# Keys of the later batches formed by channel instead of by transposing normalised tokens

## The reference

```python
k  = layernorm(x)                      # over channels; keys
# for each batch and channel, over the tokens t in order:
y  = (A*p + E*v) / (A*q + E)           # WKV recurrence with decay w and bonus u
x2 = x + tanh(g_xattn) * y
z  = layernorm(x2).astype(f16)
d  = gelu(z @ W0.T + bias0).astype(f16)   # 1024 -> 4096
e  = (d @ W1.T + bias1).astype(f16)       # 4096 -> 1024
out = x2 + tanh(g_ffn) * e
```

## Time and profile before

| | us |
|---|---|
| median of 3 runs | 1995.39 (1993.98 to 1995.86) |
| the profiled execution | 1994.41 |
| its span | 1992.6 |
| PE busy | 1856.8 (93%) |
| DVE busy | 847.7 (43%) |
| ACT busy | 549.8 (28%) |
| POOL busy | 261.9 (13%) |

### The profile page before, as it was taken

The page is one execution under the profiler, slowest core; times in us unless marked ns, Lnnn a source line. Parts: engine busy times, 40 slices in busy tenths (PEclk is TensorE's granted clock), DMA queues, the critical chain, the costliest instruction groups (busy, mean ns, idle before and its releaser), DMA issues.

```text
span 1992.6 us, 20961 instructions
## 1 busy us (share of the span) xinstructions
PE 1856.8 (93%) x8960; PEld 878.9 (44%) x8960; DVE 847.7 (43%) x998; ACT 549.8 (28%) x647; POOL 261.9 (13%) x202
## 2 busy tenths in 40 slices
PE   0069998899999999999999999999999999999999
PEld 0034444344544444444444444444444444444444
DVE  6978779686433666631223776642111000000000
ACT  3139744434422433410001443420100221210000
POOL 2335411334330011000000101000000000000000
PEclk9989999999999999999999999999999999999999
DMA  5727837578353442442233334323322222123330
GB/s 195 253 81 277 313 132 266 209 252 311 115 177 138 143 161 96 142 182 98 93 127 122 114 129 164 137 96 116 127 92 87 96 85 85 64 85 127 127 116 32
DMA packets 76748, 287.12 MB, mean 144 GB/s; under 512 B 7920, under 2 KB 7920, under 8 KB 69488
## 3 DMA queue, kind: packets, MB, share of 16 engines
q1 hardware_dynamic: 75648, 285.24, 40.5%
q10 hardware_dynamic: 1008, 0.55, 0.1%
HBM read 218.66 MB, written 67.11 MB: 143 GB/s over the span
## 4 chain that ended last, share of the span: by engine, by line
PE 81%; DVE 10%; issue 3%; DMA 3%; ACT 2%; POOL 1%; SPq 0%; ACTq 0%; DVEq 0%; POOLq 0%
PE acc L658 43%; PE acc L636 35%; DVE S L525 3%; PE front L608 1%; DVE stats L456 1%; DMA W<-parts_dram 1%; DVE S L511 1%; DVE S L514 1%; PE front L585 1%; PE back L617 1%; ACT L380 1%; POOL X L328 1%; DMA xin<-x_in 1%; DVE xin L472 1%; DMA b<-bias_in 1%
## 5 line engine op out<-in xcount | busy, mean ns | idle before, releaser
L636 PE MATMUL acc<-XT,W 128*128 128x512 f16 x4096 | 900.3, 381 | 17.5 <-DMA W<-parts_dram 12.0
L658 PE MATMUL acc<-DT,W 128*128 128x512 f16 x4096 | 892.5, 379 | 0.0
L636 PEld LDWEIGHTS acc<-XT,W 128*128 128x128 f16 x4096 | 401.6, 98 | 495.9 <-issue 13.6
L658 PEld LDWEIGHTS acc<-DT,W 128*128 128x128 f16 x4096 | 400.1, 98 | 471.6
L536 DVE SCALAR_TENSOR_TENSOR xo<-e,tg,xo 128x512 f32<-128x512 f16 x64 | 50.0, 783 | 654.3 <-ACT e L419 654.3
L411 ACT ACTIVATE DT<-acc,b 128x512 f16<-128x512 f32 x256 | 175.7, 687 | 546.1 <-PE acc L636 545.6
L419 ACT ACTIVATE e<-acc,b 128x512 f16<-128x512 f32 x64 | 43.9, 686 | 616.8 <-PE acc L658 616.8
L525 DVE RECIPROCAL S<-front 128x512 f32<-128x512 f32 x62 | 207.5, 3347 | 0.0
L328 POOL TENSOR_TENSOR X<-X,S 128x512 f32<-128x512 f32 x64 | 77.6, 1213 | 641.3 <-DVE S L528 641.3
L509 DVE TENSOR_TENSOR front<-front,V 128x512 f32<-128x512 f32 x62 | 43.2, 696 | 203.6 <-ACT front L380 203.6
L456 DVE BATCH_NORM_STATS2 stats<-front 128x6 f32<-128x512 f32 x64 | 41.4, 688 | 198.0 <-PE front L608 198.0
(11 more groups left out here) (50 smaller groups left out, 617.0 us busy)
## 6 DMA issues: line engine op xcount, KB each, us to landing
W<-parts_dram SPq DMA_DIRECT2D x56, 2048.0 KB, 8.5
parts_dram<-W SPq DMA_DIRECT2D x64, 512.0 KB, 6.1
stage<-w_in SPq DMA_DIRECT2D x52, 512.0 KB, 6.0
xin<-x_in SPq DMA_DIRECT2D x32, 512.0 KB, 6.1
V<-vT_in SPq DMA_DIRECT2D x64, 256.0 KB, 5.0
X<-xT_in SPq DMA_DIRECT2D x64, 256.0 KB, 3.0
x_dram<-X SPq DMA_DIRECT2D x32, 512.0 KB, 3.9
xo<-x_dram SPq DMA_DIRECT2D x32, 512.0 KB, 4.1
```

What stands on the lines that cost most here:

```text
L636: mm = nc.tensor.matmul(acc[m % BANKS][:, :], W[:, (nb // Q) % 2, part, nb % Q, P * c:P * (c + 1)], XT[:, c, HALF * half:HALF * (half + 1) ...
L658: mm = nc.tensor.matmul(acc[m % BANKS][:, :], W[:, s % 2, part, q, P * c:P * (c + 1)], DT[:, nb, HALF * half:HALF * (half + 1)], start=(nb ...
```

## The change

For batches 1 to 3 the key of a unit is formed from xT, which is loaded by channel anyway for the residual, and from a row that holds each token's mean and factor, the same for all partitions. The statistics are taken as before, tile by tile, but nothing is normalised by token: the pair (mean, factor) of 128 tokens is stored in a DRAM tensor, and after four tiles the row of 1024 numbers is loaded with a broadcast to all partitions, into `xin[2]` or `xin[3]`, which are free now. `keys(n)` on DVE subtracts, multiplies and adds the token-dependent term from a ramp; the different start of the second half goes into the exponential's shift. The transposes of units 16 to 63 are gone from PE. The first half's tiles of batch 1 move from slots 33 to 36 to slots 25 to 28 and the others are spread over every second slot; x is loaded two tiles ahead in two buffers; xT has eight landing semaphores instead of four. The first batch stays as it was.

```diff
     for i in range(HT):
         LN1_SLOT[HT + i] = 1 + i
-        LN1_SLOT[2 * HT + i] = 33 + i
-        LN1_SLOT[3 * HT + i] = 60 + i
+        LN1_SLOT[2 * HT + i] = 25 + i
+        LN1_SLOT[3 * HT + i] = 47 + 2 * i
...
-        LN1_SLOT[2 * TILES + i] = 107 + i
+        LN1_SLOT[2 * TILES + i] = 104 + 2 * i
...
-            LN1_SLOT[T + HT + i] = at + 33 + i
+            LN1_SLOT[T + HT + i] = at + 20 + 2 * i
             if b + 2 < B:
-                LN1_SLOT[T + TILES + i] = at + 119 + i
+                LN1_SLOT[T + TILES + i] = at + 112 + 2 * i
...
+    for n in range(UNITS, UNITS * B):
+        KEY_SLOT[n] = UNIT_SLOT[n] - 2 if n % UNITS == 0 else UNIT_SLOT[n - 1]
...
             def load_x(T):
-                half, slot = T // HT, T % HT
-                if half:
-                    sp.wait_ge(kt_done, CB * half)
+                half, slot = T // HT, T % HT if T < TILES else T % 2
+                if 0 < half < 4:
+                    sp.wait_ge(kt_done, CB * min(half, 2))
+                if T >= TILES + 2:
+                    sp.wait_ge(bn_done[0], 2 * (T - 1))
                 sp.dma_start(xin[:, slot, :], x[T]).then_inc(x_landed[slot], 16)
+
+            def store_norms(T):
+                sp.wait_ge(rstd_done[0], T + 1)
+                sp.dma_start(norms_dram[T // HT, T % HT], mv[:, 0, T % 2, :]).then_inc(norms_stored[T % 2], 16)
+
+            def load_norms(half):
+                for i in range(2):
+                    sp.wait_ge(norms_stored[i], 16 * (half - 1) * HT // 2)
+                if half >= 4:
+                    sp.wait_ge(k_ready, CB * (half - 3))
+                row = norms_dram[half:half + 1].rearrange("o a p k -> o (a p k)")
+                sp.dma_start(xin[:, 2 + half % 2, :], row.to_broadcast([P, 2 * HALF])).then_inc(norms_landed[half % 2], 16)
...
             def load_xT(n):
-                if n >= 4:
-                    sp.wait_ge(x2_done, n - 3)
+                if n >= 8:
+                    sp.wait_ge(x2_done, n - 7)
...
+                    if K - 1 in LN1_AT and LN1_AT[K - 1] >= TILES:
+                        T = LN1_AT[K - 1]
+                        store_norms(T)
+                        if T + 2 < TILES * B:
+                            load_x(T + 2)
+                        if T % HT == HT - 1:
+                            load_norms(T // HT)
...
+                    if K == LN1_SLOT[TILES]:
+                        pool.wait_ge(xn_ready, TILES)
+                        nc.gpsimd.iota(ramp, [[-1, HALF]], base=0, channel_multiplier=0, ...
...
             def exps(n):
-                act.wait_ge(kt_done, n + 1)
+                if n < UNITS:
+                    act.wait_ge(kt_done, n + 1)
+                else:
+                    act.wait_ge(k_ready, n - UNITS + 1)
...
             def stats_of(i, T, halves, free):
-                if T >= 2:
+                if i == 0 and T >= TILES + 2:
+                    dve.wait_ge(norms_stored[T % 2], 16 * ((T - TILES) // 2))
+                elif T >= 2:
                     dve.wait_ge(free, T - 1)
...
+            def keys(n):
+                b, i, c, half = n // UNITS, n % UNITS, n % CB, n // CB
+                E = unit_banks(n)[0]
+                m, r = norms[half % 2][:, :, 0], norms[half % 2][:, :, 1]
+                if i == 0:
+                    dve.wait_ge(xh_ready, TILES * b)
+                    dve.wait_ge(ramp_ready, 1)
+                else:
+                    dve.wait_ge(y_done, n - 1)
+                dve.wait_ge(xT_landed[n % 8], 16 * (n // 8 + 1))
+                dve.wait_ge(norms_landed[half % 2], 16 * (half // 2))
+                at = n - UNITS + 1
+                nc.vector.tensor_tensor(E, X2[:, i, :], m, ALU.subtract).then_inc(kc_done, 1)
+                dve.wait_ge(kc_done, at)
+                nc.vector.tensor_tensor(E, E, r, ALU.mult).then_inc(ks_done, 1)
+                dve.wait_ge(ks_done, at)
+                nc.vector.scalar_tensor_tensor(E, ramp, wp[:, c:c + 1], E, ALU.mult, ALU.add).then_inc(k_ready, 1)
...
                     if K + 1 in LN1_AT:
                         stats_x(LN1_AT[K + 1])
-                    if K in LN1_AT:
+                    if K in LN1_AT and LN1_AT[K] < TILES:
                         norm_x(LN1_AT[K])
+                    for n in KEYS_AT.get(K, ()):
+                        keys(n)
                     for n in UNITS_AT.get(K, ()):
                         unit(n)
...
             def tokens_x2(T):
-                pe.wait_ge(x2_done, UNITS * b + CB * (h + 1))
+                pe.wait_ge(x2_done, UNITS * b + (UNITS if b else CB * (h + 1)))
...
                     for n in UNITS_AT.get(K, ()):
-                        unit(n)
+                        if n < UNITS:
+                            unit(n)
```

More of the change, by code:

```diff
@@ L35 @@
 LN2_SLOT = {}
+KEY_SLOT = {}
 def place_front():
@@ L56, in place_front @@
         for i in range(HT):
-            LN1_SLOT[T + HT + i] = at + 33 + i
+            LN1_SLOT[T + HT + i] = at + 20 + 2 * i
             if b + 2 < B:
-                LN1_SLOT[T + TILES + i] = at + 119 + i
+                LN1_SLOT[T + TILES + i] = at + 112 + 2 * i
         for i in range(TILES):
             LN2_SLOT[T + i] = (at + 72 + 6 * i, at + 75 + 6 * i)
+    for n in range(UNITS, UNITS * B):
+        KEY_SLOT[n] = UNIT_SLOT[n] - 2 if n % UNITS == 0 else UNIT_SLOT[n - 1]
 place_front()
 UNITS_AT = {k: [n for n in UNIT_SLOT if UNIT_SLOT[n] == k] for k in set(UNIT_SLOT.values())}
+KEYS_AT = {k: [n for n in KEY_SLOT if KEY_SLOT[n] == k] for k in set(KEY_SLOT.values())}
 LN1_AT = {k: T for T, k in LN1_SLOT.items()}
@@ L88, in build @@
     x2_view = x2_dram.rearrange("b (h c) p u t -> b c u p h t", h=2)
+    norms_dram = nc.dram_tensor("norms_dram", (2 * B, HT, P, 2), F32).ap()
     parts_dram = nc.dram_tensor("parts_dram", (2 * STEPS, P, 2 * Q * 1024), F16).ap()
@@ L108, in build @@
         w_u, wn, decay = sb("w_u", [P, 2, CB]), sb("wn", [P, CB]), sb("decay", [P, CB])
-        wp, uu, bonus, shift = sb("wp", [P, CB]), sb("uu", [P, CB]), sb("bonus", [P, CB]), sb("shift", [P, CB])
+        wp, uu, bonus, shift = sb("wp", [P, CB]), sb("uu", [P, CB]), sb("bonus", [P, CB]), sb("shift", [P, 2, CB])
         grow = sb("grow", [P, H])
@@ L113, in build @@
         xin = sb("xin", [P, HT, H])
+        norms = [xin[:, 2 + i, :].rearrange("p (t k) -> p t k", k=2) for i in range(2)]
+        ramp = grow[:, 0:HALF]
         stats, mv, rstd = sb("stats", [P, 2, 2, 6]), sb("mv", [P, 2, 2, 2]), sb("rstd", [P, 2, 2, 2])
@@ L139, in build @@
         xn_done, xn_ready, xh_ready = sem("xn_done"), sem("xn_ready"), sem("xh_ready")
+        norms_stored, norms_landed, ramp_ready = sems("norms_stored"), sems("norms_landed"), sem("ramp_ready")
+        kc_done, ks_done, k_ready = sem("kc_done"), sem("ks_done"), sem("k_ready")
         kt_done, e_ready, y_done, x2_done = (sem(n) for n in ("kt_done", "e_ready", "y_done", "x2_done"))
@@ L180, in load_xT @@
                     sp.wait_ge(x2_stored[(b - 1) % 2], 16 * CB * ((b - 1) // 2 + 1))
-                sp.dma_start(X2[:, i, :], xT[b, i]).then_inc(xT_landed[n % 4], 16)
+                sp.dma_start(X2[:, i, :], xT[b, i]).then_inc(xT_landed[n % 8], 16)
             def store_x2(n):
@@ L282, in _ @@
                             store_x2(n - 1)
-                        if n % CB == CB - 1 and (n + 1) // CB < 2 * B:
-                            for T in range((n + 1) // CB * HT, ((n + 1) // CB + 1) * HT):
+                        if n == UNITS - 1:
+                            for T in range(TILES, TILES + 2):
                                 load_x(T)
@@ L319, in rstd_of @@
                 pool.wait_ge(ve_done[i], T + 1)
-                nc.gpsimd.tensor_tensor(rstd[:, i, T % 2, 1:2], rstd[:, i, T % 2, 0:1], power[:, :], ALU.pow)\
+                to = mv[:, 0, T % 2, 1:2] if i == 0 and T >= TILES else rstd[:, i, T % 2, 1:2]
+                nc.gpsimd.tensor_tensor(to, rstd[:, i, T % 2, 0:1], power[:, :], ALU.pow)\
                     .then_inc(rstd_done[i], 1)
@@ L325, in residual @@
                 pool.wait_ge(y_done, n + 1)
-                pool.wait_ge(xT_landed[n % 4], 16 * (n // 4 + 1))
+                pool.wait_ge(xT_landed[n % 8], 16 * (n // 8 + 1))
                 slot = X2[:, n % UNITS, :]
@@ L349, in _ @@
                         rstd_of(0, LN1_AT[K + 1])
+                    if K == LN1_SLOT[TILES]:
+                        pool.wait_ge(xn_ready, TILES)
+                        nc.gpsimd.iota(ramp, [[-1, HALF]], base=0, channel_multiplier=0,
+                                       allow_small_or_imprecise_dtypes=True).then_inc(ramp_ready, 1)
                     if K in X2T_AT:
@@ L374, in exps @@
             def exps(n):
-                act.wait_ge(kt_done, n + 1)
+                if n < UNITS:
+                    act.wait_ge(kt_done, n + 1)
+                else:
+                    act.wait_ge(k_ready, n - UNITS + 1)
                 if n == 0:
                     act.wait_ge(s_dve0, 6)
```

(13 more changed lines are left out.)

2 lines of the change are left out of this document (1 added, 1 removed).

## The result

The changed kernel takes 2004.59 us (median of 5 runs, 2004.06 to 2008.80) against 1995.39 (5 runs, 1992.79 to 1995.93): a ratio of 1.0055, 95% interval 1.0040 to 1.0069, so 0.55% slower. The profiled execution took 2006.68, its span is 2004.9.

A forecast was written before the change was run, and what follows sets the result against it. The prediction took TensorE as the bound (81% of the chain), with DVE holding it up in batch 0. Batch 0 17.7 us later less 16.7 saved gave +1.0, so 1996 us; range 1981 to 2013.

The forecast's parts named there:

- Batches 1 and 2: Later batches: removed transposes (14.1 us) and two waits for keys (2.6) save 16.7 us, 8.3 per batch; DVE's passes stay hidden.
- The port: SBUF port in each unit: DVE's first keys pass starts 0.04 us ahead of GpSimd's residual and wins, at no cost.
- the rival: GpSimd wins the port: first keys pass ends 1.08 us later, +14, about 2010; 25% together with slow passes.
- Slots 24 to 37: Batch 0: moved statistics and x loads make tile 4 5.3 us late, PE 8.7 late; slot 37 at 282.7.
- Slots 37 to 64: Batch 0: DVE without a gap, units 10.9 us apart; weights put slot 60 at 382.3, slot 64 at 398.6.
- Slots 64 to 88: From slot 64 of batch 0: DVE's gaps used up; tokens_x2(8) starts at 489.9, PE waits 8.4 us, clock costs 2.7.
- My fourth case: Something else is late too, a lo_piece before keys passes or the row of means: 2015 and above, 7%.
- The sum: Whole kernel: batch 0 17.7 us later, less 16.7 saved, is +1.0 us; forecast by the median 1996.
- the 498 named as the limit: Sign of being wrong: slot 88 comes by 480 or after 498 us.
- the stall of batch 0: Batch 0 up to slot 88: the change makes it 15.0 us later, before 2.7 more for the clock.
- the lost port: Case of GpSimd winning the port, or slow keys passes: about 2010 us, slower than before, 25%.
- a rival of 6 to 8 us: Smaller stall of batch 0: slot 60 and all behind it 6 to 8 us earlier, about 1987; 28%.

The follow-up runs named there:

- e2: The kernel before with eight landing semaphores for xT instead of four and nothing else: 1977.06 us against 1994.81, ratio 0.9912.
- e1: The changed kernel with keys by channel for batches 2 and 3 only, batch 1's by transposes at the old slots: 1963.77 us, ratio 0.9845.
- e6: The changed kernel with one more, unused DVE keys pass per unit in batches 2 and 3 only: 2004.58 us, ratio 1.0047.
- e8: The changed kernel with the wait for the unit before (`y_done`) named last instead of first in `keys`: 2011.06 us, ratio 1.0076.
- e11: The changed kernel with batch 1's keys formed in one pass, mean and factor left out, the wait for their row kept: 1995.83 us, ratio 1.0009.
- e3: The changed kernel with x of tiles 8 to 11 loaded at once into four buffers: 1998.43 us, ratio 1.0019.
- e4: The changed kernel with batch 0's weight loads issued ahead of the V loads in the SP queue: 1998.07 us, ratio 1.0021.
- e12: The changed kernel with the edits of e11, e3 and e4 together: 1984.43 us, ratio 0.9949.
- e5: The changed kernel with one more, unused DVE keys pass per unit in batch 1 only: 2014.54 us, ratio 1.0095.
- e7: The changed kernel with x of tiles 8 to 11 loaded at once and their statistics at slots 31 to 34: 2000.89 us, ratio 1.0028.

## Why the prediction was right or wrong

**Batches 1 and 2: right.** Predicted 16.7, less 2.7 for the clock behind slot 88, so 14.0 from `tokens_x2(8)` to the end; measured 15.15, and PE waits for nothing there. The two batches gained 9.0 and 8.0 (8.3 each was predicted), the clock behind slot 88 cost 1.8. The transposes are 7.0 of it in each batch (459.57 in e2, 452.59 in e1); the two waits are gone in e2 too, where the keys are as before, so the semaphores alone remove them. e6 shows that DVE's passes are hidden.

**The port: right.** DVE wins at a lead of 0.04 in the ordinary unit, and e8 shows the price if it does not: 6.5, about half of the 14 of the rival. The Trainium skill's rule (SBUF — State Buffer, "Who interferes with whom"), that whichever is issued first keeps the ports, agrees with 298.90 and 298.94 here, and with e8. It doesn't agree with e11, where the instruction that starts 0.04 earlier by the trace is the one held up; there the measurement decides. Of the two rows that the prediction held against the rule, the copy has only one SBUF input, so the part on two inputs says nothing of it.

**Slots 24 to 37: right in kind, short in size.** Tile 4 was to be 5.3 late; the rows of after run 1.4 earlier before this point (unit 15 ends at 229.87 against 231.24; in e2 tile 4 is 1.8 earlier, so the semaphores do that), and 236.52 - 232.74 + 1.4 is 5.2. Slot 29 was to be at 250.1 and came at 252.96: the loads of tiles 10 and 11 took 7.0 and 10.1 us, not 5.4. I had taken 5.4 from batch 1, where no weights are prepared; the chain of after shows the load (start us, us, what):

```profile
237.39 10.08 DMA xin<-x_in
```

Behind the 6 us wait the granted clock fell (0.52 from 253 to 257 us; it cost 1.9), which I had counted only at slots 60 and 88. Slot 37 came at about 287.4 instead of 282.7.

**Slots 37 to 64: right, with small terms too low.** Unit period 10.96 against 10.9. The waits of the slots before 60 (8.35 at 348.70) are contained in the lateness of slot 60, as predicted. The row of means cost 5.2 us of DVE instead of 3.2, and the weights 9.9 from issue to landing instead of 9.2 (DVE and, of the chain, the DMAs of the kernel after):

```profile
376.81 0.70 DVE L554 TENSOR_TENSOR front<-X,xin 128x512 f32<-128x512 f32 x1 [5.21 <-DMA xin<-norms_dram]
```

```profile
365.98 6.35 DMA norms_dram<-mv
372.39 4.31 DMA xin<-norms_dram
380.78 9.92 DMA W<-parts_dram
```

Slot 60 came at 390.75 instead of 382.3, slot 64 at 407.5 instead of 398.6.

**Slots 64 to 88: a term missing.** 3.6 us more than predicted. The queued output addition and `lo_piece` each take the port away from DVE. The addition (442.25) stands between unit and keys, so the residual, at 442.42 in the POOL rows above, is queued ahead of the keys pass and not behind it; and the seed copy meets `lo_piece`. DVE of the kernel after:

```profile
442.25 0.74 DVE L603 SCALAR_TENSOR_TENSOR xo<-e,tg,xo 128x512 f32<-128x512 f16 x1
442.91 1.59 DVE L554 TENSOR_TENSOR front<-X,xin 128x512 f32<-128x512 f32 x1
...
457.05 1.81 DVE L574 COPY S<-state 128x2 f32<-128x2 f32 x1
```

Three such passes at +0.9 and three copies at +2.5 together: 5.3. Units of the second half repeat at 10.7 instead of 10.55, another 0.9. Against that the prediction counted a set of keys too many: behind unit 24 it took seven units with keys, but only six keys stand there (the last at 479.94), 2.1 less. That makes 4.1, against the 3.6 seen. My fourth case had `lo_piece`, but not the additions.

**The sum.** Slot 88 at 502.37 instead of 489.9, 12.5 off and past the 498 named as the limit; that statement of the prediction failed. The failing step is the stall of batch 0, 15.0, which measured 27.45 in the traces (some 24 by the medians). By e3 the late x is worth 6 us, by e4 the weights behind V 6.5; the two nearly add up (11.4 from e11 to e12). How the rest of the 40.8 splits stays open in part. e12, without two of the three passes, x early and weights first, still takes 20.7 more than e1. What is left in it is the wait for residual(15), the row of means and the single pass that loses the port; I did not measure the three apart. By the traces e12 is behind e1 by 4.6 at tile 4, 7.5 at slot 32, 11.2 at slot 60, 10.4 at slot 64 and 18.3 at slot 88.

**Luck.** That the kernel became slower was given 40%, but mostly for the lost port (25%), which did not come in the ordinary unit. It came by a longer stall of batch 0, a case that I had not named beyond `lo_piece` and the row of means. The range held because it was wide enough for that.

**The eight semaphores: misjudged.** I named them only as a point for a rival of 6 to 8 us, and the sum has no term for them. Alone they are worth 17.7, more than all the transposes of batches 2 and 3, and by that they cover part of the loss in batch 0: 27.45 us against the kernel before, 39.8 against e1. The change with four semaphores was not run, so what they give inside it isn't measured.

## What to carry to other kernels

Take a change that comes in parts apart before it is judged: here a gain of 31 us (1963.77 against 1994.8) was hidden under a loss of 40.8, because the same edit was also made in batch 0, where DVE and the queue behind it are the bound. In this kernel a pass added on DVE was free where its unit still fits under the matmuls, and cost its full length elsewhere; one added pass per stretch (e5, e6) tells which. On an in-order DMA queue look at what each wait holds back: four more landing semaphores gave 17.7 us, the transposes taken away in batches 2 and 3 13.3.

## What the runs showed of the hardware

- The order in which the waits were written decided a race: a DVE instruction held by its first wait starts 0.04 us behind the releaser's end, held by its third 0.14 (e8), and POOL's residual 0.08 (298.86 to 298.94). That alone was 6.5 us.
- A SCALAR_TENSOR_TENSOR with two SBUF inputs lost the port though it started 0.04 ahead, and took 1.87 (e11); a TENSOR_TENSOR with the same lead kept it, 0.70. With a lead of 0.16 a SCALAR_TENSOR_TENSOR (with one f16 input) kept it too, 0.74.
- A 1 KB store in the company of 2 MB loads took 6.35 us here and 8.63 in e7, and set the time.
- A factor read at every second element cost nothing: 0.70 (299.63), against 0.69 for dense rows (306.03).
- Behind PE's waits of 6 to 12 us the granted clock was 0.50 (1.2 GHz) for a while, which cost 1.6 to 3 us each: four slots took 16.94 us at 390.75, behind a wait of 12.11, and 13.99 at 364.65, behind one of 0.16.
